# An attention and routed-experts kernel: output bias by ScalarE into PSUM, up biases read in place, epsilon added by GpSimd

## What is computed

```python
x = x + attention(layernorm(x))
# experts, for the rows xf of layernorm(x); F = 512
h = gelu(xf @ Wi_e + bi_e, approximate=False) * sigmoid(xf @ Wg_e + bg_e)
r = xf + (h @ Wo_e + bo_e)
mu, var = mean(r), mean((r - mu) ** 2)            # over the 128 columns
y_e = (r - mu) * rsqrt(var + 1e-12) * gamma_e + beta_e
x = x + sum over the row's two experts of  weight * y_e
```

## Time and profile before

| | |
|---|---|
| median of 3 runs | 1165.48 us (1165.04 to 1169.55) |
| the profiled execution | 1167.83 us, its span 1165.7 us |
| PE busy | 1065.2 us (91% of the span), 8520 products |
| DVE busy | 978.4 us (84%) |
| ACT busy | 790.4 us (68%) |
| POOL busy | 759.1 us (65%) |

### The profile page before, as it was taken

How to read it: one execution, slowest core, us unless ns; L and a number is a source line. 1 busy time by engine, 2 the same in 40 slices (tenths; PEclk the granted TensorE clock), 3 DMA queues, 4 the chain that set the end, 5 groups by cost and what they waited for, 6 DMA issues and landing times. The chain is left out here.

```text
span 1165.7 us, 27224 instructions
## 1 busy us (share of the span) xinstructions
PE 1065.2 (91%) x8520; PEld 811.9 (70%) x8520; DVE 978.4 (84%) x2727; ACT 790.4 (68%) x1806; POOL 759.1 (65%) x1377
## 2 busy tenths in 40 slices
PE   2899899999999999999999999799999999999910
PEld 1566665666666666666666665599999999999910
DVE  4776888888888888888888877689999999999959
ACT  1466666766766666666766766788888888888800
POOL 2257565877877776776676666557678777777730
PEclk9999999999999999999999999999999999999965
DMA  5324356445345344345344334722122221211048
GB/s 138 109 62 144 97 172 191 119 141 181 114 143 184 113 120 154 95 121 155 108 120 142 105 111 112 229 79 65 56 80 78 58 56 56 57 54 56 27 150 305
DMA packets 142877, 135.74 MB, mean 116 GB/s; under 512 B 72360, under 2 KB 96944, under 8 KB 142736
## 3 DMA queue, kind: packets, MB, share of 16 engines
q1 hardware_dynamic: 131792, 111.98, 32.7%
q0 software_dynamic: 8640, 17.84, 4.6%
q10 hardware_dynamic: 2304, 4.20, 0.9%
HBM read 75.33 MB, written 58.62 MB: 115 GB/s over the span
## 5 line engine op out<-in xcount | busy, mean ns | idle before, releaser
L1103 ACT ACTIVATE probs<-st 128x384 f32<-128x384 f32 (+1 forms) x768 | 377.1, 524 | 216.6 <-PE st L887 210.6
L1294 DVE TENSOR_REDUCE neg_max<-sa 128x2 fp32r<-128x1024 f32 (+3 forms) x384 | 388.7, 1037 | 74.3 <-PE sa L872 71.3
L804 POOL TENSOR_SCALAR_AFFINE_SELECT probs<-probs 128x128 f32<-128x128 f32 (+1 forms) x768 | 241.2, 333 | 175.6 <-ACT probs L1103 170.4
L887 PE MATMUL st<-q_stack,k_pad 128*128 128x256 f32 (+2 forms) x1024 | 305.0, 371 | 6.0 <-ACT probs L1103 2.8
L867 PE MATMUL sa<-k_pad,q_stack 128*128 128x256 f32 (+2 forms) x1024 | 277.5, 348 | 20.5 <-DMA k_pad<-k_scratch 14.6
L887 PEld LDWEIGHTS st<-q_stack,k_pad 128*128 128x128 f32 x1024 | 165.4, 190 | 63.2 <-ACT probs L1103 43.7
L867 PEld LDWEIGHTS sa<-k_pad,q_stack 128*128 128x128 f32 x1024 | 167.3, 192 | 48.1 <-DMA k_pad<-k_scratch 20.9
L830 POOL DMA_INDIRECT y_scratch<-z,to_row x142 | 171.5, 1208 | 35.9 <-issue 35.9
L900 PE MATMUL pv<-probs,v_aug 128*32 128x512 f32 (+3 forms) x2048 | 167.7, 439 | 0.1
L935 PE MATMUL up<-xt_hi,w_cur 128*128 128x256 f32 x568 | 166.3, 293 | 1.4 <-ACT hid L1029 1.0
L936 PE MATMUL up<-xt_lo,w_cur 128*128 128x256 f32 x568 | 160.7, 283 | 0.0
(11 more groups left out here) (176 smaller groups left out, 1443.0 us busy)
## 6 DMA issues: line engine op xcount, KB each, us to landing
q_stack<-q_scratch SPq DMA_DIRECT2D x64, 256.0 KB, 2.7
k_pad<-k_scratch SPq DMA_DIRECT2D x256, 64.0 KB, 2.5
xg<-rows_scratch SPq DMA_DIRECT2D x71, 130.0 KB, 2.2
q_scratch<-q_hi SPq DMA_DIRECT2D x16, 512.0 KB, 3.1
k_scratch<-k_hi SPq DMA_DIRECT2D x16, 512.0 KB, 2.9
y<-y_scratch SPq DMA_DIRECT2D x16, 512.0 KB, 5.5
q_scratch<-q_lo SPq DMA_DIRECT2D x17, 256.0 KB, 3.2
k_scratch<-k_lo SPq DMA_DIRECT2D x17, 256.0 KB, 3.3
```

The source lines that it names most:

```text
L804: pool.affine_select(out=blk, in_=blk, compare_op=ALU.is_ge, fill=0.0, base=0, pattern=[[0, w], [1, P]], channel_multiplier=-1).then_inc(m ...
L887: last = nc.tensor.matmul(st[:, t % 2, at:at + w], k_pad[:, G * g + j, kk * P:(kk + 1) * P], q_stack[:, g, S - w:S], start=True, stop=True)
L1103: nc.scalar.activation(probs[:, n % 2, j, lo:lo + w], st[:, k % 2, at:at + w], ACT.Exp).then_inc(exp_done, 1)
L1294: V.tensor_reduce(neg_max[:, n % 2, heads[0]:heads[-1] + 1, i], scores[:, :, 0:(i + 1) * P], AX.X, ALU.max, negate=True).then_inc(sa_read, 1)
```

## The change

The output bias of a block is no longer written by a product on PE. A new tile `bo_sb` holds every expert's bias in all partitions, filled in the two places of the attention stage that GBa and GBb had (now BOa and BOb). In each step ACT copies the expert's part of it into `y_ps`, when the residual of the block before has read it, and signals `bo_done`; `down` waits for that. This function, `output_bias`, stands last in ACT's list. The four fills of gamma and beta are all between steps now: two after step 0, one each after steps 1 and 2. The activations take their bias from `b_up` at an offset in a register, and DVE's copy into `b_cur` is gone. The addition of epsilon moves from DVE to POOL, ahead of the power. Some waits on tiles that now lie elsewhere in memory are added or moved with it.

```diff
-            -2: "... XG S5 B10 RC B11 WC WO GBa EX ON",
-            -1: "PV0 E0 PV1 Rb PV2 PV3 GBb E1 OT RC ON",
+            -2: "... XG S5 B10 RC B11 WC WO BOa EX ON",
+            -1: "PV0 E0 PV1 Rb PV2 PV3 BOb E1 OT RC ON",
...
-            0: "Rc- AR GBc S6--", 1: "GBd S7--", 2: "Rd- PD out", ...
+            0: "Rc- AR GBa GBb S6--", 1: "GBc S7--", 2: "GBd Rd- PD out", ...
...
             def deviation(s, u):
+                pool.wait_ge(x_chain, 2 * s + 2)
+                r = u % NR
+                pool.tensor_scalar(inv_dev[:, r, :], mean_var[:, r, :, 1], EXPERT_EPS, None, ALU.add).then_inc(ve_done, 1)
                 pool.wait_ge(ve_done, s + 1)
...
             def down(s, u):
                 pe.wait_ge(hid_done, 2 * s + 2)
-                if not before(s, 1):
-                    pe.wait_ge(res_done, s)
-                nc.tensor.matmul(y_ps[:, :, :], b_sel[:, bass.ds(e * P, P)],
-                                 b_stack[:, 0:D].unsqueeze(1).broadcast_to([P, 2, D]), start=True, stop=True)
+                pe.wait_ge(bo_done, s + 1)
...
-                        bias = b_cur[:, u % 2, m, c:c + 1]
+                        bias = b_up[:, m, bass.ds(e * FC + c, 1)]
...
+            def output_bias(s, u):
+                e = expert_of(u)
+                if s == 0:
+                    act.wait_ge(gb_done, len(BO_STEPS))
+                if not before(s, 1):
+                    act.wait_ge(res_done, s)
+                nc.scalar.activation(y_ps[:, :, :], bo_sb[:, bass.ds(e * D, D)].unsqueeze(1).broadcast_to([P, 2, D]),
+                                     ACT.Copy).then_inc(bo_done, 1)
...
-            step, steps = stages([(-1, copy_weights), (0, activations), (-2, load_expert), (-2, high_x)])
+            step, steps = stages([(-1, copy_weights), (0, activations), (-2, load_expert), (-2, high_x), (0, output_bias)])
...
-                V.tensor_copy(b_cur[:, u % 2, :, :], b_up[:, :, bass.ds(e * FC, FC)])
...
-            def add_epsilon(s, u):
-                dve.wait_ge(x_chain, 2 * s + 2)
-                V.tensor_scalar(inv_dev[:, u % NR, :], mean_var[:, u % NR, :, 1], EXPERT_EPS, None, ALU.add)\
-                    .then_inc(ve_done, 1)
...
             step, steps = stages([(-1, copy_weights), (3, scale), (2, mean_and_variance), (3, shift),
-                                  (2, add_epsilon), (0, product), (-2, load_expert), (1, residual), (-2, low_x),
+                                  (0, product), (-2, load_expert), (1, residual), (-2, low_x),
                                   (1, row_statistics)])
```

More of the change, by code:

```diff
@@ L271, in schedule @@
                             yield kind, int(token[len(kind):] or 0), b
-        GB_STEPS = ("GBa", "GBb", "GBc", "GBd")
+        BO_STEPS, FACTOR_STEPS = ("BOa", "BOb"), ("GBa", "GBb", "GBc", "GBd")
+        GB_STEPS = BO_STEPS + FACTOR_STEPS
         def guests():
@@ L343, in pe_sequence @@
                 pe.wait_ge(r_const, made["b_stack, b_sel"])
-                for half in range(2):
-                    e = 2 * GB_STEPS.index(kind) + half
+                for half in range(2 if kind in FACTOR_STEPS else 0):
+                    e = 2 * FACTOR_STEPS.index(kind) + half
                     last = nc.tensor.matmul(misc[:, half * 2 * D:(half + 1) * 2 * D], b_sel[:, e * P:(e + 1) * P],
                                             b_stack[:, D:3 * D], start=True, stop=True)
+                for quarter in range(4 if kind in BO_STEPS else 0):
+                    e = 4 * BO_STEPS.index(kind) + quarter
+                    last = nc.tensor.matmul(misc[:, quarter * D:(quarter + 1) * D], b_sel[:, e * P:(e + 1) * P],
+                                            b_stack[:, 0:D], start=True, stop=True)
                 last.then_inc(misc_written, 1)
@@ L363, in act_sequence @@
             elif kind in GB_STEPS:
-                i = GB_STEPS.index(kind)
+                i = GB_STEPS.index(kind) - (len(BO_STEPS) if kind in FACTOR_STEPS else 0)
                 act.wait_ge(misc_written, misc_use(kind, n))
                 act.wait_ge(st_written, NB_ * GROUPS_ALL)
-                nc.scalar.activation(gb_sb[:, i * 4 * D:(i + 1) * 4 * D], misc[:, :], ACT.Copy).then_inc(gb_done, 1)
+                act.wait_ge(pv_written, GROUPS_ALL - 1)
+                made_ = gb_sb if kind in FACTOR_STEPS else bo_sb
+                nc.scalar.activation(made_[:, i * 4 * D:(i + 1) * 4 * D], misc[:, :], ACT.Copy).then_inc(gb_done, 1)
         def dve_sequence(dve, kind, k, n):
@@ L506, in attention_and_routed_experts @@
         to_row = sb("to_row", [P, NX, 2], I32)
-        b_cur = sb("b_cur", [P, 2, 2, FC])
         st6 = sb("st6", [P, 2, 2, 6])
@@ L511, in attention_and_routed_experts @@
         xt_hi = sb("xt_hi", [P, 2, BR], F32R)
-        between = sb("between", [P, 288])
+        between = sb("between", [P, 304])
         w_hi = [wi_hi, sb("wg_hi", [P, E * F], F32R)]
@@ L517, in attention_and_routed_experts @@
         gb_sb = sb("gb_sb", [P, E * 2 * D])
+        bo_sb = sb("bo_sb", [P, E * D])
         xt_lo = sb("xt_lo", [P, 2, BR], F32R)
@@ L536, in attention_and_routed_experts @@
         z_done, x_chain, z_chain = sem("z_done"), sem("x_chain"), sem("z_chain")
+        bo_done = sem("bo_done")
         def rounds(s, n, each):
@@ L839, in _ @@
                         pool.wait_ge(on_done, GROUPS_ALL)
+                        for stored in on_stored:
+                            pool.wait_ge(stored, 16 * 2 * BATCHES)
                         pool_const(pool, pool.memset(pads[:, :, :, :], 0.0))
@@ L1018, in activations @@
             def activations(s, u):
+                e = expert_of(u)
+                if s == 0:
+                    act.wait_ge(b_up_done, 1)
                 if not before(s, 2):
@@ L1125, in copy_weights @@
                     dve.wait_ge(hi_loaded, 16 * 2 * E)
-                    dve.wait_ge(b_up_done, 1)
                     dve.wait_ge(pv_written, GROUPS_ALL - 1)
@@ L1182, in scale @@
                     dve.wait_ge(scattered[r], rounds(s - NR, NR, 32))
+                dve.wait_ge(x_chain, 2 * s + 2)
                 for h in range(2):
```

4 lines of the change are left out of this document (2 added, 2 removed), and 3 rows, old and new, of tables (GUESTS, LAST_SLOTS).

## The result

The changed kernel takes **1217.11 us** (median, 1215.45 to 1217.17) against 1165.26 us (1161.86 to 1169.55) of the kernel before: a ratio of 1.0438, 95% interval 1.0414 to 1.0462. The forecast was 1216 us (1199 to 1235) and slower. Its profiled execution has a span of 1215.1 us, 49.4 more than before; the forecast's sum was +50.5.

What follows compares the result with a forecast made beforehand. PE was taken to bound the kernel at 5.00 us a block, with a 5.77 us ring of waits replacing it. Stage +51.3, fills -1.75 and end +1 gave +50.5 on the median 1165.48: 1216 us, range 1199 to 1235.

Steps and rivals of the forecast that it cites:

- The ring: Bias copy, weight copies, activations, second product, to_row, residual, back to bias copy: 5.77 us a step (5.58 to 5.94), against 5.00.
- The hand-over: From the end of DVE's residual to the start of ACT's bias copy: 0.23 us (0.05 to 0.29).
- the copy: ACT's copy of 256 columns of output bias into y_ps: 0.28 us (0.27 to 0.39).
- The signs named in the prediction: Changed profile: blocks about 5.8 us, ACT waiting for DVE's residual, PE idle about 0.9, DVE over 1 before second product.
- The stage: Activations of block 2 to block 69: 67 steps of 5.77 plus 5 of late ACT work, 391.6 us, 51.3 more.
- the similar work on DVE: Late batch's work on DVE, 0.7 to 1.5 us in a few steps, fits into DVE's wait for ACT.
- The factor fills: Moved fills at step 0 remove PE's 3.50 us idle stretch and keep its clock up: -1.75 us (between 0 and that).
- The end: Last step: shorter ring, but the last down waits for product, residual and bias copy: +1 us for both (0 to 2).
- The register instructions ahead of the activations: Forecast hidden on ACT; rival, not hidden: 0.37 us more a step, 1241 us, 7 in 100.
- The product's worth: Bias product gone from PE: 71 products of 0.12 us give PE back 8.5 us.
- That PE stays the bound: Rival: only the products leave the path, with a ring shorter than PE's new 4.88 us step: 1157 us, 4 in 100.
- The fallen clock: Rival: PE, idle about 0.89 us each step, drops to half clock, about 9.5 us a step: about 1465, 3 in 100.

Runs made afterwards that it cites:

- e2: Changed kernel with only the output bias by ACT and its fills; up-bias copy and epsilon addition back on DVE: 1217.4 us, ratio 1.0445.
- e1: Changed kernel with the output bias again a product on PE, the rest of the change kept: 1162.03 us, ratio 0.9983.
- e8: Changed kernel with no output bias at all, neither product on PE nor copy on ACT: 1154.3 us, ratio 0.9906.
- e7: Changed kernel with the next block's weight copies put ahead of ACT's bias copy and its wait: 1159.6 us, ratio 0.9958.
- e5: Changed kernel with a second, unread ACT copy ahead of the wait for the residual in 67 steps: 1210.2 us, ratio 1.0381.
- e9: Changed kernel with an extra ACT copy ahead of the wait, read at a constant offset without a register: 1216.0 us, ratio 1.0458.
- e6: Changed kernel with a second, unread ACT copy behind the wait and the bias copy in 67 steps: 1232.9 us, ratio 1.0576.
- e3: Changed kernel with ACT's bias copy one step later, behind the first bank of the next block's activations: 1167.0 us, ratio 1.0023.

## Why the prediction was right, step by step

**The ring.** Its old pieces were forecast at 5.26 and measure 5.24; they did not change by being waited for. The hand-over was put at 0.23 (0.05 to 0.29) and is 0.13; the copy was put at 0.28 (0.27 to 0.39) and is 0.32. These two misses partly cancel: 5.77 forecast, 5.69 measured. The Trainium skill, page "ScalarE: Activation LUTs", section "What ACT_TABLE_LOAD costs", gave an estimate of 0.306 for the copy; the measured 0.32 is nearer to that than to the 0.28 taken from xt_hi. The hand-over was taken from PE, whose rows with a register instruction had 0.24; PE itself still takes 0.23 here (1102.99 + 0.39 to PEld's start at 1103.61), so in these rows the size goes with the engine that is woken, and the row of another engine was only a bound. The signs named in the prediction are there, two of them smaller: PE's row shows 0.57 idle and not 0.9, though from its last up product (1102.77) to its first down product (1103.62) it is 0.85, where it was 0.12; and DVE waits 0.77 ahead of its second product and not over 1, because another 0.39 now falls ahead of its first.

**The stage.** Forecast 391.6, measured 388.37 (761.53 to 1149.90):

```profile
761.53 0.83 ACT L1041 ACTIVATE hid<-up,b_up 128x256 f32<-128x256 f32 x2
...
1149.90 0.82 ACT L1041 ACTIVATE hid<-up,b_up 128x256 f32<-128x256 f32 x2
```

67 steps at 5.695 are 381.6, so the late work costs 6.8 and not the 5 forecast. The four steps that hold ACT's late work are longer by 5.4 together: none of it was overlapped, which is 0.4 of the missing 1.8. The step that failed is that the similar work on DVE "fits into its wait for ACT". That wait is 0.39 + 0.77 = 1.16 in a step, near the 1.18 forecast, but the forecast's own "0.7 to 1.5 us" is more than that at its upper end. In the worst step the late work holds DVE for 1.79 (920.33 to 922.12) ahead of both products, 0.63 more than the wait takes up, and ACT's wait grows by just this, from 1.05 to 1.68:

```profile
926.15 0.39 ACT L1053 ACTIVATE y_ps<-bo_sb 128x256 f32 x1 [1.68 <-DVE res L1176]
```

Three such steps (waits of 1.24, 1.34 and 1.68) make up 1.1 of the 1.8.

**The factor fills.** This term was wrong: -1.75 forecast, -0.39 measured (block 2 starts at 761.53 instead of 761.92). Of that, +0.33 lies ahead of the stage, whose start differs by several us between kernels; from block 0's activations to block 2's it is 13.18 instead of 13.90, so -0.72. I said that the long idle stretch would be gone and the clock stay up. The stretch only moved. Timeline of ACT and PE:

```profile
748.51 0.38 PE L347 MATMUL misc<-b_stack,b_sel 128*128 128x256 bf16 x2
...
751.48 0.45 ACT L1053 ACTIVATE y_ps<-bo_sb 128x256 f32 x1
751.79 0.66 ACT L374 ACTIVATE gb_sb<-misc 128x512 f32<-128x512 f32 x1
752.50 0.39 PE L347 MATMUL misc<-b_stack,b_sel 128*128 128x256 bf16 x2 [3.61 <-ACT gb_sb L374]
...
757.14 1.95 PE L960 MATMUL y_ps<-wo_sb,hid 128*128 x16
```

and the windows at the same place:

```profile
754.00:757.00 3.00, 3.00 (x16) 3.00 (x16) 1.34 (x3) 2.82 (x8) 0.00 (x0) 0.50 0.20 41
757.20:759.00 1.80, 1.80 (x18) 1.80 (x18) 0.69 (x2) 0.84 (x2) 0.00 (x0) 1.00 0.53 84
```

The second fill waits 3.61 us for ACT to empty `misc`, and that copy stands on ACT behind all activations of block 0. The down products do take 1.95 instead of 3.70, as forecast, but the half clock (0.50, the level of 1.2 GHz) now falls on the up products of block 1 ahead of them. I had counted the wait, and not asked where PE would be idle meanwhile.

**The end.** +1 forecast; from block 69's activations to the end of the span it is 65.20 us instead of 63.51, +1.69. What that term missed is the clock. Timeline of PE, and a window there:

```profile
1159.52 3.59 PE L960 MATMUL y_ps<-wo_sb,hid 128*128 x16 [2.61 <-ACT y_ps L1053]
```

```profile
1160.00:1162.00 2.00, 2.00 (x10) 2.00 (x11) 0.70 (x3) 0.00 (x0) 1.69 (x3) 0.50 0.05 12
```

PE stands idle 2.61 us for the last bias copy, and its last 16 products run at 0.50, in 3.59 us where the last ones before took 2.05, starting 0.12 after a bias product that had waited 0.74. In e2, after the same idle time (2.60), these products took 2.12, and from block 69 to the end it is 64.06: so it is the clock that costs here, more than the wait, and it does not fall at the same moment in each kernel's profile.

The parts together: 48.10 - 0.39 + 1.69 = 49.4, against 51.3 - 1.75 + 1 = 50.5. That the sum came so close is in part luck: the stage is 3.2 below its forecast, and the two small terms are 2.0 above theirs.

**What cost nothing.** The register instructions ahead of the activations are hidden, as forecast: the activations still start 0.36 apart (1104.35, 1105.06, 1105.78 and 1106.49 for two each). Epsilon takes POOL 0.34, more than the nearest row's 0.20, and POOL waits 1.79 ahead of it. The product's worth, forecast at 8.5 us, measures 8.3 by e1 and e8, though nobody gets it as long as the ring is there.

**The clock in the stage.** It stayed at 1.00 through an idle 0.57 in every regular step. In one step it fell: two table loads on ACT made PE wait 2.37 us for a bank of `up`, and from 832.25 on its up products start 0.21 apart in place of 0.12. Window and timeline of PE there:

```profile
820.00:835.00 15.00, 11.64 (x85) 11.21 (x86) 11.27 (x41) 12.85 (x30) 9.88 (x12) 0.91 0.17 51
```

```profile
830.76 0.36 PE L947 MATMUL up<-xt_hi,w_cur 128*128 128x256 f32 x1 [2.37 <-ACT hid L1041]
```

The step is 2.92 longer than a regular one, and ACT's late work accounts for all of it, so the slower products cost nothing there.

**The rivals.** That PE stays the bound was given 4 in 100 and decided at a ring below 4.88 us. e7 is that case: with a ring of 4.65 its step is 4.83, and the time 1159.6 against the 1157 that the rival gave. The register instructions ahead of the activations, 7 in 100, were hidden as forecast; the one that had a price stands between ACT's wait and the bias copy, inside the hand-over. The fallen clock, 3 in 100, came in single places and not in every step.

## What to carry to other kernels

Before a wait is moved from one engine to another, add up the path from the waiting instruction round to what it waits for: if that ring, with the new work in it, is longer than the bound engine's step, it becomes the step, and no engine will look full. Work whose input is ready early (here the weight copies) belongs ahead of the wait and not behind it; that alone turned 4.4% slower into 0.4% faster. A ring somewhat shorter than that step still keeps an engine from catching up (e7). Where a wait ends a ring, have the register arithmetic done ahead of it.

## What the runs showed of the hardware

- A register instruction of 46 ns that carries a wait on ACT costs 0.09 to 0.10 us between the end of DVE's work and the start of ACT's: 0.03 without it (e5), 0.12 to 0.13 with it (changed kernel, e9). Ahead of an activation that waits for nothing it costs nothing.
- ACT's copy of 256 columns takes 0.32 us from start to start into PSUM and 0.30 into SBUF (e6).
- When PE's wait for the bias ends only as it needs it, its down products take 2.05 in place of 1.95: the first weight load starts together with them and not ahead (e3, 1055.40). In e7, where the bias is there 0.9 us earlier, it is loaded ahead.
- POOL's power of 128x2 mostly took 0.72 us in the changed kernel and 1.28 in e1 and e7 with the same instruction (1.09 before); 0.72 is the shortest in each of them. What sets this stays open.
